# A graph layer on one core: SyncE fetches one source tile of every fifth block row by row, in GpSimd's place

## The reference

```
h = relu(layernorm(x))
Q = h @ W_Q.T ;  K = h @ W_K.T
score = (Q[dst] . K[src]) / sqrt(128) * exp(-edge_weight)
keep the 16 best edges of each target; alpha = softmax of their scores
agg[n] = sum over the kept edges of alpha * (h[src] @ W_msg.T)
out = x + relu(h @ W_self.T + agg)
```

## Time and profile before

| | |
|---|---|
| median of 3 runs | 2013.98 us (2013.44 to 2015.44) |
| the profiled execution: its own time, its span | 2014.03 us, 2011.8 us |
| busy: DVE, POOL, PE, ACT | 74%, 74%, 70%, 53% of the span |
| gathers on POOL (L615) | 1564, 948 ns each in the three large groups |
| mean granted TensorE clock | 0.867 |

### The profile page before, as it was taken

One profiled execution on the slowest core, in us unless ns is written; L12 is line 12 of the kernel. 1 busy time (PEld: TensorE's weight loads), 2 busy tenths in 40 slices (PEclk: granted clock), 3 DMA queues, 4 the chain that ended last, 5 costly groups with the idle time before them and its releaser, 6 DMA issues. The chain is left out here.

```text
span 2011.8 us, 45575 instructions
## 1 busy us (share of the span) xinstructions
PE 1403.0 (70%) x15219; PEld 1289.3 (64%) x15220; DVE 1487.9 (74%) x5024; ACT 1074.5 (53%) x3376; POOL 1491.9 (74%) x1577
## 2 busy tenths in 40 slices
PE   1157888777767777676777767677767767677776
PEld 0157888766666666666667666666766766666665
DVE  6668999777677767767676777767777776767766
ACT  2767676554545545454554545455454545555453
POOL 7777777777777777777777777777777777777773
PEclk9968989888888898888888888888888888898888
DMA  8933333333333333333323333333333333333321
GB/s 232 281 95 88 115 106 116 102 89 99 102 86 102 88 100 94 95 102 84 103 86 102 89 99 100 88 102 88 100 96 92 97 91 101 86 102 89 97 74 33
DMA packets 120604, 205.86 MB, mean 102 GB/s; under 512 B 32268, under 2 KB 75922, under 8 KB 120172
## 3 DMA queue, kind: packets, MB, share of 16 engines
q0 software_dynamic: 50112, 102.80, 20.1%
q1 hardware_dynamic: 69627, 97.27, 14.9%
q10 hardware_dynamic: 626, 2.84, 0.4%
HBM read 186.34 MB, written 16.44 MB: 101 GB/s over the span
## 5 line engine op out<-in xcount | busy, mean ns | idle before, releaser
L615 POOL DMA_INDIRECT X<-H_table,idx x662 | 627.3, 948 | 202.7 <-issue 198.7
L1138 ACT ACTIVATE X<-OT,w 128x125 f32<-128x125 bf16 x1792 | 530.0, 386 | 30.8 <-DVE w L955 30.8
L615 POOL DMA_INDIRECT E<-H_table,idx x437 | 414.4, 948 | 136.4 <-issue 130.6
L1106 ACT ACTIVATE OT<-pT 128x512 bf16<-128x512 f32 (+1 forms) x500 | 274.7, 549 | 423.8 <-PE pT L1242 414.2
L615 POOL DMA_INDIRECT Z<-H_table,idx x403 | 382.0, 948 | 123.0 <-issue 119.9
L1242 PE MATMUL pT<-identb,O 125*128 125x128 bf16 x1800 | 211.2, 243 | 270.2 <-DVE X L876 251.0
L1242 PEld LDWEIGHTS pT<-identb,O 125*128 125x128 bf16 x1800 | 135.7, 108 | 319.7 <-issue 269.7
L1231 PE MATMUL pG<-G,O 125*128 125x128 bf16 x3600 | 314.6, 250 | 0.0
L1231 PEld LDWEIGHTS pG<-G,O 125*128 125x128 bf16 x3600 | 276.1, 115 | 0.1
L881 DVE TENSOR_REDUCE s<-X 128x8 f32<-128x1024 f32 x200 | 268.6, 1343 | 0.0
L1267 PE MATMUL pU<-X 128*128 128x125 f32 x1512 | 191.7, 282 | 1.6
(11 more groups left out here) (197 smaller groups left out, 2523.1 us busy)
## 6 DMA issues: line engine op xcount, KB each, us to landing
rawi<-D_table SPq DMA_DIRECT2D x50, 576.0 KB
ewt<-D_table SPq DMA_DIRECT2D x50, 576.0 KB
X<-H_table,idx POOLq DMA_INDIRECT x662
E<-H_table,idx POOLq DMA_INDIRECT x437
Z<-H_table,idx POOLq DMA_INDIRECT x403
hb<-H_table SPq DMA_DIRECT2D x100, 62.5 KB
xb<-in_x SPq DMA_DIRECT2D x100, 62.5 KB
out<-ob SPq DMA_DIRECT2D x100, 62.5 KB
```

What stands on the lines that cost most here:

```text
L615: return eng.indirect_dma_start(out=Et[q][:, t * 128:(t + 1) * 128], out_offset=None, in_=x if b < RAW else H, in_offset=bass.IndirectOffs ...
L1106: AT.mark(eng.activation(OT[b % 3][:, q0[g]:q0[g] + GQ[g], :].rearrange("p t n -> p (t n)"), pT[:, 0:GQ[g] * 128], ACT.Copy), b, f"T{g}")
L1138: last = eng.activation(weighted(c)[:, t * 128:t * 128 + NB], OT[c % 3][:, t, 0:NB], ACT.Copy, scale=w[:, t:t + 1])
```

## The change

For the blocks 8, 13, ..., 98 (`owned`, 19 blocks) POOL leaves out the gather of tile 14 (OWN). SP fetches this tile instead. For that the source numbers are copied once, as integers, into a table `SRC` in HBM: two DMAs from the input and one of zeros (`ms`, cleared by a new small memset on DVE) for its padding. In five rounds that follow each other, k = 0 to 4, SP serves block b = j + 5 - k. For k = 0 it loads the block's start into a register, fetches the tile's 128 numbers into `own`, and waits until the buffer is free ("agg3" and "cp" of block b - 7) and the numbers are there. Then in each of the rounds one instruction loads 26 numbers (24 in the last) into registers, and for each number one DMA copies one row of H (512 bytes) into one partition of the tile. All of a tile's DMAs count on `s_row[0]` or `s_row[1]` in turn; who waited for the gather of tile 14 now waits for 128 x 16 counts there. This is DVE before its last product and POOL before tile 6 of the next block.

```diff
+    OWN = 14
+    EVERY = 5
+    FROM = 8
+    PER = 26
...
+        def owned(b):
+            return FROM <= b < B and (b - FROM) % EVERY == 0
+
+        def owned_before(b):
+            return len([c for c in range(b) if owned(c)])
+
         def landed(eng, b, t):
             if b >= 0:
                 k = t % AHEAD
-                eng.wait_ge(s_gp[k], 16 * ((1 if k < 2 else 2) * b + t // AHEAD + (0 if k == 1 else 1)))
+                if t == OWN and owned(b):
+                    n = owned_before(b)
+                    eng.wait_ge(s_row[n % 2], 16 * 128 * (n // 2 + 1))
+                else:
+                    less = owned_before(b) if k == OWN % AHEAD else 0
+                    eng.wait_ge(s_gp[k], 16 * ((1 if k < 2 else 2) * b + t // AHEAD + (0 if k == 1 else 1) - less))
...
+            for p, q in RUNS:
+                eng.dma_start(SRC[0, 0:M].rearrange("(p r) -> p r", r=RUN)[p:q, :], src2[p:q, :]).then_inc(s_sc, 16)
+            VS.wait(eng, "msz")
+            eng.dma_start(SRC[0, M:MP].rearrange("(t e) -> t e", e=128), ms[:, :]).then_inc(s_sc, 16)
             meta(LEAD + 1)
             load_h(2)
             spread(2)
+
+            def own_rows(b, k):
+                n = owned_before(b)
+                if k == 0:
+                    if n == 0:
+                        eng.wait_ge(s_sc, 48)
+                    r = eng.value_load(alrow[0:1, b:b + 1], min_val=0, max_val=M)
+                    eng.dma_start(own[:, :], SRC[0:1, bass.ds(r + OWN * 128, 128)]).then_inc(s_own, 16)
+                    PM.wait(eng, b - NE, "agg3")
+                    AC.wait(eng, b - NE, "cp")
+                    eng.wait_ge(s_own, 16 * (n + 1))
+                lo, hi = PER * k, min(PER * (k + 1), 128)
+                _, rows = nc.values_load_multi_w_load_instructions(own[0:1, lo:hi], engines=[mybir.EngineType.SP], min_val=0, max_val=N - 1,
+                                                                     skip_runtime_bounds_check_because="source nodes of the input")
+                for p in range(lo, hi):
+                    eng.dma_start(Et[b % NE][p:p + 1, OWN * 128:(OWN + 1) * 128],
+                                  H[bass.ds(rows[p - lo], 1), :]).then_inc(s_row[n % 2], 16)
+
             for j in range(B):
...
+                for k in range(EVERY):
+                    if owned(j + EVERY - k):
+                        own_rows(j + EVERY - k, k)
                 load_x(j)
...
                 for t in range(1 if b else 0, SURE):
+                    if t == OWN and owned(b):
+                        continue
...
+            VS.wait(eng, "msf")
+            VS.mark(eng.memset(ms[:, :], 0), "msz")
```

More of the change, by code:

```diff
@@ L66, in gnn_kernel @@
     CP = [1, 1, 1, 1, 1, 5]
+    OWN = 14
+    EVERY = 5
+    FROM = 8
+    PER = 26
     H = nc.dram_tensor("H_table", [N, D], f32, kind="Internal").ap()
     D16 = nc.dram_tensor("D16_table", [1, MP], i16, kind="Internal").ap()
+    SRC = nc.dram_tensor("SRC_table", [1, MP], i32, kind="Internal").ap()
+    HF = H.rearrange("n d -> (n d)")
     META = nc.dram_tensor("META_table", [4, MP], f32, kind="Internal").ap()
@@ L132, in gnn_kernel @@
         cprow = sb("cprow", [1, 128], i32)
+        own = sb("own", [1, 128], i32)
         MR = [sb(f"MR{q}", [128, 128]) for q in range(NM)]
@@ L245, in gnn_kernel @@
         s_relay = sem("s_relay")
+        s_sc = sem("s_sc")
+        s_own = sem("s_own")
+        s_row = [sem(f"s_row{q}") for q in range(2)]
         s_fl = sem("s_fl")
@@ L298, in gnn_kernel @@
         shares = ["rstd", "nmr", "n", "h"]
-        vn = ["zero", "ident", "identb", "mr0", "msf", "pad16", "pad", "rawd", "neq", "c1", "winr", "win", "wini", "val", "scan",
+        vn = ["zero", "ident", "identb", "mr0", "msf", "pad16", "pad", "msz", "rawd", "neq", "c1", "winr", "win", "wini", "val", "scan",
               "ctmp", "carry", "slot", "cnt2", "rb", "rbrow", "rbf", "al", "alf", "step", "cp"]
```

## The result

The changed kernel takes 2053.61 us (median of 4, 2053.09 to 2054.90), the kernel before on the same chip 2014.71 us (2013.44 to 2015.52): a ratio of 1.0196 (95%: 1.0184 to 1.0209), 39 us slower. Forecast were 2043 us and a range of 2026 to 2255. The profiled execution took 2053.37 us.

The account below looks back on a forecast made before the run. The prediction took POOL, full at one gather per 1.248 us, as the bound: a wait before block 9's tile 6 ending 51.6 us later, less 22.5 for gathers saved, gives +29.1, hence 2043.1 us; range 2026 to 2255.

Parts of the forecast that it names:

- The bound and the gain: POOL is full at 1.248 us a gather; 19 fewer give 23.7 us, 22.5 of them behind block 9's wait.
- The place of the wait: POOL stands once, before gather t = 6 of block 9 near 203 us, for SP's rows; none from block 13 on.
- Its length: POOL's wait at block 9 ends at 255.9 us, 51.6 later than the 204.33 at which that gather began.
- I take 1.2: one trip of 0.64 and 0.02 for each of 25 neighbouring words: Assumed price in us of SP's one instruction loading 26 registers; bounds 0.44 and 16.7.
- the TENSOR_LOAD of own at 1 to 2 us: Sign to look for on SP: how long each load of the tile's numbers into registers would last.
- 2037 + 5L: Forecast time in us while POOL's one wait at block 9 decides, with five register loads in the chain before it.
- L: Price in us of SP loading 26 registers by one instruction; taken as 1.2, shown by no row.
- SP becomes the bound: Rival: with slow register loads POOL waits for SP at every owned block, from L = 3.5 on; chance 0.39.
- 1719.6 + 95L: Time in us if SP's own chain of 95 rounds bounds the whole run; decides from L = 3.5 on.
- What costs nothing: Claim that the copy of src, a small DVE memset and SP's later load_x, spread and load_h are free.
- load_x, spread and load_h come up to 12 us later in a round, and are used two rounds on: Claim that these SP transfers, delayed by the added work, cost nothing.
- Rows in time: faster: Rival: POOL does not stall at block 9, so all 23.7 us stay, 1990 us; chance 0.02.

Follow-up runs that it names:

- e2: Changed kernel without SP's row fetches and the waits for them, so nobody fetches tile 14 of the 19 blocks: 1989.64 us, ratio 0.9876.
- e8: Changed kernel with the first owned block 18 instead of 8 and all register loads starting at a multiple of four words: 1992.86 us, ratio 0.9895.
- e4: Changed kernel with the first owned block 23 instead of 8, so 16 owned blocks: 1998.66 us, ratio 0.9918.
- e1: Changed kernel, but POOL's tile 6 gather behind an owned block no longer waits for SP's rows; DVE still does: 2039.92 us, ratio 1.0123.
- e3: Changed kernel, but POOL keeps all its gathers and SP's rows go to a spare buffer: 2046.85 us, ratio 1.0154.
- e6: Changed kernel with the 128 numbers one word further on in own, so no load starts at a multiple of four words: 2178.87 us, ratio 1.0814.
- e5: Changed kernel with the 128 numbers cut so that all register loads start at a multiple of four words: 2043.78 us, ratio 1.0143.
- e7: As e3, but 13 rows a round instead of 26, for every tenth block from 13 on: 2014.98 us, ratio 1.0004.

## Why the prediction was right, and where it was off

**The bound and the gain** held. POOL was full, and a gather was worth its 1.248 us: e2 gave 24.9 us for 19, e8 22.0 for 17. In e4 only 15.8 of 20.0 came. Summed over POOL's timeline from 600 us on, the steps above 1.248 us make 6.5 us in the kernel before, 5.3 in e2 and 6.6 in e8, but 10.5 in e4, 11.1 in e1 and 11.2 in e3 (8.8 in the changed kernel, which is 2.3 of its missing 2.8). Those with more carry long loads, and with e5's short ones it is 7.1. But e6, whose loads are all long, has 6.0 us in steps of less than 1 us too much, and the changed kernel 8.0; so the long loads do not explain it, and the cause is open.

**The place of the wait** held: the sum put it before t = 6 of block 9, once, near 203 us, and nowhere later, and so it was.

**Its length was mis-sized**, 263.3 instead of 255.9. By the terms of the sum: the loads took 16.7 us instead of 6.0 (+10.7), the 128 rows 52.7 instead of 57.6 (-4.9), the landing before POOL's gather 1.2 instead of 2.3 (-1.1; the last row was issued by 262.11), and the rounds' own DMAs, the register steps and a later start together +2.7. The term that failed is "I take 1.2: one trip of 0.64 and 0.02 for each of 25 neighbouring words"; with it failed the sign "the TENSOR_LOAD of own at 1 to 2 us" for the loads of 5.5 us. The formula around it had the right parts: 2037 + 5L with the measured L of 3.33 gives 2053.8 us. That this meets 2053.6 so closely is luck: rows and landing took 6.0 us less than its terms, the other parts of the rounds 2.7 and POOL's small steps 2.8 more.

**SP becomes the bound**, at 0.39 the largest rival, was the right mechanism for longer loads. With L = 3.5 as the threshold and 3.33 measured the changed kernel lies just below, and e6, with L = 5.4, is above it. By the measured rounds the point lies higher, at an estimated 4.1 (93.2 us with L = 3.33, and 97.0 to fill). For e6 the formula 1719.6 + 95L gives 2233, 54 too much, because the rows were cheaper (19 x 4.9 = 93 us less) and the other parts dearer.

**What the Trainium skill said** on register loads ("Runtime: NRT & Kernel Launch", Instruction fetch mechanics: about 200 ns per register even in bulk, there from HBM) is what a load from SBUF paid in this trace where its start was no multiple of four words, 5.47 us for 26. The loads of 26 that start at such a multiple took 2.04 us, less than half. By that figure alone the time would have been an estimated 2255 us; with both kinds of load in the kernel it was 2053.6. The floor of 600 ns that the Trainium skill gives in "DMA: Bandwidth & Descriptors", Latency and other measured facts, and that the prediction says agrees with 0.644, agrees with this median only: the same rows have 0.437 us at least on SP, and 0.290 in the middle on POOL.

**"What costs nothing"** was wrong on one point: "load_x, spread and load_h come up to 12 us later in a round, and are used two rounds on". In the changed kernel it hardly showed: PE's one late wait for hb, 5.9 us, fell into POOL's gap. But e3, in which nobody waits for the rows, had hb late at 26 places and lost 32 us. Delays of one round add up when SP's round is longer than DVE's. The copy of src cost nothing that e2 could show.

**"Rows in time: faster"** (0.02) was rightly small: with this order on SP it cannot be. e1 shows more, that most of the lead would have been lost without that wait too.

## What to carry to other kernels

An engine that is the bound may live on a lead early in the run, and a helper must be measured against the pace of that stretch, which is the pace of the others (14.3 us a round here) and not the bound's (19.5): the same change that loses 39 us from block 8 on gains 16 from block 23 on (e4), and with short loads 22 from block 18 on (e8). Before giving an issuing queue more work, sum its whole round and compare it with the shortest round that it serves; everything it issues after the new work comes later by all of it, and the backlog adds up. Where registers are loaded in bulk, let each load start at a multiple of four words.

## What was not expected of the hardware

- A load of 26 registers on SP from one SBUF row took 2.04 us where its start was a multiple of four words and 5.47 where it was not: by the estimate above about 0.20 us a step on top of 0.3 to 0.4 us, a step being four words in the one case and one word in the other. One register took 0.66 us on SP and 0.29 on POOL.
- SP issued a DMA of one 512-byte row in 0.228 us, 0.41 with its register steps. 1152 of them that nobody waited for cost the others nothing measurable (e7: 1.0004, 0.9994 to 1.0014). The last row of a tile released DVE 1.0 us after its issue (262.11 to 263.07), while DVE's wait for a gather ended 2.6 us after the gather's end.
- On one chip the kernel before took 3227 us instead of 2014, and the runs there show PE pausing between its own instructions; the cause is not known.
